# A two-attention, two-expert-layer block on one core: five steps moved around the expert layers, and the row maxima of the second attention handed over by PSUM bank

## What is computed

```python
x = x + attn_a(layernorm(x))
x = x + ffn(layernorm(x))
x = x + attn_b(layernorm(x))
x = x + ffn(layernorm(x))
```

```python
probs = softmax(q @ k.T)                      # 16 maps of 256 x 256
diff = probs[:, :, 0] - lam * probs[:, :, 1]
attn = (diff @ v) * rsqrt(mean(attn * attn) + 1e-5) * (1 - LAMBDA_INIT)
```

## Time and profile before

| | us |
|---|---|
| median of 3 runs | 936.07 (934.92 to 939.77) |
| the profiled execution, its own time | 938.77 |
| its span in the profile | 936.9 |
| PE busy | 830.4 (89%) |
| DVE busy | 697.6 (74%) |
| POOL busy | 573.9 (61%) |
| ACT busy | 555.4 (59%) |
| TensorE clock granted, mean | 0.947 |

### The profile page before, as it was taken

How to read it: one execution, slowest core, us unless ns; L and a number is a source line. 1 busy time by engine, 2 the same in 40 slices (tenths; PEclk the granted TensorE clock), 3 DMA queues, 4 the chain that set the end, 5 groups by cost and what they waited for, 6 DMA issues and landing times.

```text
span 936.9 us, 21558 instructions
## 1 busy us (share of the span) xinstructions
PE 830.4 (89%) x6976; PEld 578.8 (62%) x6976; DVE 697.6 (74%) x1916; ACT 555.4 (59%) x888; POOL 573.9 (61%) x666
## 2 busy tenths in 40 slices
PE   2799999987899999998789898898868889999998
PEld 1455555544687777787455555555534577777786
DVE  7588777785677777775778988889874587777764
ACT  1688887874544444444478888888864444444443
POOL 4677766681566676746347675767632776666652
PEclk8899999997999999999599999999985799999999
DMA  7000000001122222230000000000001122333331
GB/s 210 17 2 2 2 1 0 1 2 46 47 91 91 92 91 91 89 92 1 1 2 4 2 1 1 1 1 1 3 2 47 46 86 96 103 101 96 99 109 40
DMA packets 35702, 42.35 MB, mean 45 GB/s; under 512 B 5936, under 2 KB 18992, under 8 KB 35632
## 3 DMA queue, kind: packets, MB, share of 16 engines
q1 hardware_dynamic: 34048, 40.85, 14.3%
q10 hardware_dynamic: 1584, 0.62, 0.2%
HBM read 38.83 MB, written 2.36 MB: 44 GB/s over the span
## 4 chain that ended last, share of the span: by engine, by line
PE 49%; DVE 22%; POOL 11%; issue 10%; ACT 4%; DMA 3%; DVEq 1%; ACTq 0%; POOLq 0%
PE psum L1375 9%; DVE s_mxs L1137 6%; PE psum L394 6%; PE psum L1337 4%; PE psum L1338 4%; PE psum L1339 4%; DVE f_xe L1502 4%; PE psum L857 3%; POOL s_inv L1091 3%; PE psum L825 3%; PE psum L364 3%; PE psum L425 3%; PE psum L380 2%; PE psum L1393 2%; POOL s_rot L1106 2%
## 5 line engine op out<-in xcount | busy, mean ns | idle before, releaser
L1460 POOL TENSOR_TENSOR f_xe_lo<-f_xe,f_xe_hi 128x512 fp32r<-128x512 f32 x96 | 123.5, 1287 | 145.6 <-ACT f_xe_hi L1434 145.6
L1434 ACT ACTIVATE f_xe_hi<-f_xe 128x512 fp32r<-128x512 f32 x128 | 80.8, 631 | 207.9 <-DVE f_xe L1502 207.9
L1137 DVE TENSOR_REDUCE s_mxs<-psum 128x4 fp32r<-128x1024 f32 x128 | 155.8, 1219 | 30.4 <-PE psum L842 29.0
L1518 DVE TENSOR_TENSOR f_h<-psum,f_g 128x512 f32<-128x512 f32 x144 | 99.1, 688 | 88.4 <-ACT f_g L1419 70.2
L1375 PEld LDWEIGHTS psum<-w,f_h 128*128 128x128 f32 x1152 | 146.0, 191 | 29.7 <-DVE f_h L1518 21.4
L998 ACT ACTIVATE s_probs<-psum 128x1024 f32<-128x1024 f32 x128 | 131.2, 1025 | 50.0 <-PE psum L825 48.4
L1375 PE MATMUL psum<-w,f_h 128*128 128x128 f32 x1152 | 157.1, 279 | 3.8 <-DVE f_h L1518 2.5
L495 ACT ACTIVATE s_probs<-psum 128x1024 f32<-128x1024 f32 x128 | 126.0, 1023 | 28.8 <-PE psum L380 28.2
L1337 PE MATMUL psum<-f_xe_hi,w_hi 128*128 128x512 f32 x288 | 127.0, 441 | 1.1 <-POOL f_xe_lo L1460 1.1
L1338 PE MATMUL psum<-f_xe_hi,w_lo 128*128 128x512 f32 x288 | 114.4, 397 | 0.0
L1339 PE MATMUL psum<-f_xe_lo,w_hi 128*128 128x512 f32 x288 | 113.9, 396 | 0.0
(11 more groups left out here) (179 smaller groups left out, 1557.9 us busy)
## 6 DMA issues: line engine op xcount, KB each, us to landing
f_gt<-gates SPq DMA_DIRECT2D x128, 256.0 KB, 3.2
x<-in_x SPq DMA_DIRECT2D x8, 256.0 KB, 6.0
out<-x SPq DMA_DIRECT2D x8, 256.0 KB, 2.3
w<-in_w SPq DMA_DIRECT2D x3, 512.0 KB, 5.7
s_qt<-s_mt SPq DMA_DIRECT2D x32, 8.0 KB
rope_cos<-in_rope_cos SPq DMA_DIRECT2D x1, 256.0 KB, 3.6
rope_sin<-in_rope_sin SPq DMA_DIRECT2D x1, 256.0 KB, 3.5
gates<-f_sg SPq DMA_DIRECT2D x16, 16.0 KB
```

The source lines that it names most:

```text
L1137: dve.tensor_reduce(mxs[:, km % 2, p, r:r + 2, :, c:c + 1].bitcast(F32R), room(km, i).rearrange("p (r j s) -> p r j s", r=2, j=2), AX.X, A ...
L1460: pool.tensor_tensor(xe_lo[:, ring(e), :], src, xe_hi[:, ring(e), :], ALU.subtract).then_inc(xe_lo_pool.sem, 1)
```

## The change

Six edits:

1. **Maxima by bank.** PE writes the four products of a block bank by bank (u = 0, then u = 1) instead of half of each bank at a time, waits for DVE per bank, and signals each bank. DVE reduces each bank of 512 columns with an instruction of its own (two columns of `s_mxs`), 256 instructions instead of 128. The wait of PE for DVE moves from ahead of the block into it.
2. **LEAD, FF_LEAD.** The first lead-in slots (e = 0 to 4) stand after slots 2, 8, 10, 12, 14 of the last step but one instead of 5, 7, 9, 11, 13; x_turn moves from e = 0 to e = 1. So `f_xn` stands after slot 2 and `x_turn` after slot 8; both stood after slot 5.
3. **ACT in the expert layer.** The copy `f_xt` stands ahead of the high part `f_xe_hi` in the same slot.
4. **Normalising a chunk.** Three of the four `f_xn` in slot 3 and one in slot 4, instead of two and two.
5. **preceding** stands at slot 5 of step 0 of the second attention instead of slot 14 of step -1.
6. The semaphore counts that follow from 1.

```diff
-    mx_mm, mx_sb, mt_mm, mt_sb = ev("mx_mm", PAIRS), ev("mx_sb", PAIRS), ev("mt_mm", 2), ev("mt_sb", 2)
+    mx_mm, mx_sb, mt_mm, mt_sb = ev("mx_mm", 2 * PAIRS), ev("mx_sb", 2 * PAIRS), ev("mt_mm", 2), ev("mt_sb", 2)
...
-                pe.wait_ge(mx_sb.sem, mx_sb.upto(m, i - 1 if km == 0 and i else i))
-
-            def maxima(m, km, i, j):
-                c, q = i // 2 % 2, 2 * (i // 4) + j
-                for u in range(2):
+            def maxima(m, km, i, u):
+
+                pe.wait_ge(mx_sb.sem, mx_sb.upto(m, 2 * (i - 1 if km == 0 and i else i) + u - 1))
+                c = i // 2 % 2
+                for j in range(2):
+                    q = 2 * (i // 4) + j
                     r, o = 32 * (2 * (i % 2) + u), 512 * u + SEQ * j
                     ins = pe.matmul(room(km, i)[:, o:o + SEQ], qt[r:r + 24, km % 2, q, c * P:(c + 1) * P],
                                     kt[r:r + 24, km % 2, q, :], start=True, stop=True)
...
                     for m, km, i in blocks:
-                        ins = maxima(m, km, i, c)
-                        if c == 1:
-                            ins.then_inc(mx_mm.sem, 1)
+                        maxima(m, km, i, c).then_inc(mx_mm.sem, 1)
...
-                dve.wait_ge(mx_mm.sem, mx_mm.upto(m, i + 1))
-
-                dve.tensor_reduce(mxs[:, km % 2, p, r:r + 2, :, c:c + 1].bitcast(F32R),
-                                  room(km, i).rearrange("p (r j s) -> p r j s", r=2, j=2),
-                                  AX.X, ALU.max, negate=True).then_inc(mx_sb.sem, 1)
+                for u in range(2):
+                    dve.wait_ge(mx_mm.sem, mx_mm.upto(m, 2 * i + u + 1))
+                    dve.tensor_reduce(mxs[:, km % 2, p, r + u, :, c:c + 1].bitcast(F32R),
+                                      room(km, i)[:, 512 * u:512 * u + 512].rearrange("p (j s) -> p j s", j=2),
+                                      AX.X, ALU.max, negate=True).then_inc(mx_sb.sem, 1)
...
-LEAD = {(NSEQ - 2, 5): (0,), (NSEQ - 2, 7): (1,), (NSEQ - 2, 9): (2,), (NSEQ - 2, 11): (3,), (NSEQ - 2, 13): (4,),
+LEAD = {(NSEQ - 2, 2): (0,), (NSEQ - 2, 8): (1,), (NSEQ - 2, 10): (2,), (NSEQ - 2, 12): (3,), (NSEQ - 2, 14): (4,),
...
-FF_LEAD = {"x_turn": 0, "xt_sb": 1, "logits": 2, "best": 2, "index": 2, "masks": 2, "exp": 4, "sums": 4, "gates": 4}
+FF_LEAD = {"x_turn": 1, "xt_sb": 1, "logits": 2, "best": 2, "index": 2, "masks": 2, "exp": 4, "sums": 4, "gates": 4}
...
-                for m, km, next_e in inputs(n, k, e):
-                    high(m, km, next_e)
...
                     act.activation(xt[:, km % 2, :], T, ACT.Copy).then_inc(xt_sb.sem, 1)
+                for m, km, next_e in inputs(n, k, e):
+                    high(m, km, next_e)
...
-                    normalise(n + 2, (0, 1) if e == FF["norm"][0] else (2, 3))
+                    normalise(n + 2, (0, 1, 2) if e == FF["norm"][0] else (3,))
...
-            if n == -1 and h == 14 and preceding:
+            if n == 0 and h == 5 and preceding:
```

More of the change, by code:

```diff
@@ L885, in max_turn @@
             def max_turn(m, km, p):
-                pe.wait_ge(mx_sb.sem, mx_sb.upto(m, 4 * p + 4))
+                pe.wait_ge(mx_sb.sem, mx_sb.upto(m, 8 * p + 8))
                 if km + 1 < NSEQ:
```

## The result

The changed kernel takes **904.96 us** (median of 4 runs, 903.96 to 908.1) against 936.46 us for the kernel before on the same chip (4 runs, 934.92 to 939.77): ratio 0.9663, 95% interval 0.964 to 0.9687, so 31.5 us faster. The forecast was 904.0 with 891 to 924. The profiled execution took 905.03 us (span 902.7, mean granted clock 0.968), where the one before took 938.77. Lines of the code have moved by one: L825 stayed, the PE lines behind it up to the output projection are one higher (the maxima's products went from L842 to L843), all that follow are one lower (L998 is now L997, L1387 is L1386). Of the 11 executions of the kernel before in the second set of experiments one, of 2496.32 us at a granted clock of 1.00, is not compared with anything.

What follows compares the result with a forecast made beforehand. No one engine bounds the whole: PE bounds the expert layers, POOL's chain with DVE the second attention's loop. Terms -12 - 11 - 5 - 1 + 1 - 4 = -32 from 938.8 give 906.8, less 2.7: 904 us, range 891 to 924.

Steps and rivals of the forecast that it cites:

- a clock of 0.50 again between the last scores and the first experts: Sign of being wrong: half clock at the second seam, between second attention and second expert layer, in the profile after.
- Expert layers, -12: Both expert layers: PE's waits for f_xn and f_xt vanish in 12 chunk preparations, saving 12 us.
- Full removal is 12 x 1.15 = 13.8 us: Expert layers: upper end of the gain, 1.15 us of PE waits in each of 12 chunks; the lower end is 0.
- Second seam, -11: Lead into the second expert layer: without PE's gap the clock can stay up, saving 11 us; ends -2 and -15.
- a granted clock of 1.00 through the second: Sign of being right: PE's clock stays at full rate through the lead into the second expert layer.
- the clock falls again: Rival, 22%: the clock drops at the second seam, whose lead keeps about 3 of 11 us; 912 us total.
- First seam, -5: Lead into the first expert layer: less of 4.33 us PE idle and half-clock work, saving 5 us; ends 0 and -8.
- It now stands ahead of it: Lead into the first expert layer: f_xn, which took 3.82 us, now precedes POOL's 2.61 us w_lo.
- Start of the second attention, -1: Moving preceding shortens PE's 2.21 us idle before the first scores, saving 1 us; ends +1 and -3.
- Maxima in the loop, +1: Second attention's loop: split reductions against earlier PE work cost 0.1 us in each of 10 steps, +1 us.
- Maxima outside the loop, -4: About 20 second-attention blocks can fall from 1.95 to 1.66 us, saving 4 us; ends -6 and +1.
- The slower rival: Rival, 5%: bank order makes PE the bound in the second attention's loop; at 0.8 us more per block, 950 us.

Runs made afterwards that it cites:

- b_chunk: Kernel before with only the earlier f_xt copy and the three-and-one f_xn split in the expert layers: 919.70 us against 938.92, ratio 0.9791.
- b_copy: Kernel before with only ACT's f_xt copy put ahead of the high part, f_xn left two and two: 928.60 us against 936.42, ratio 0.9928.
- b_lead: Kernel before with only the LEAD and FF_LEAD slots changed: 926.67 us against 938.92, ratio 0.9858.
- a_wlo: The changed kernel with GpSimd's second w_lo moved from slot 5 to slot 15 of step 14, first attention: 902.22 us against 934.62 before, ratio 0.9641.
- change_again: The changed kernel itself, timed again beside the kernel before: 905.28 us against 934.62, ratio 0.9679.
- b_prec: Kernel before with only preceding moved to slot 5 of step 0 of the second attention: 935.70 us against 938.92, ratio 0.9978.
- a_rstd: The changed kernel with GpSimd's second-attention rstd moved from slot 14 to slot 3 of the next step: 899.46 us against 934.62 before, ratio 0.9624.
- b_bank: Kernel before with only the maxima handed over by bank and the counts for it: 934.42 us against 938.92, ratio 0.9938.

## Why the prediction was right, and where it was not

The sum was -32 us against the profiled execution; that one came out 33.7 shorter, the medians 31.5. The two largest gains came by the mechanisms named, but the terms were off in opposite directions: the expert layers gave some 5 us more than the sum has, the two seams some 7 less. That the sum came within 2 us is in part luck. One of the prediction's own signs of being wrong, "a clock of 0.50 again between the last scores and the first experts", did appear (0.57 on average over 703 to 715, so half clock for 10.3 of 12 us). Of its signs of being right, PE idle under 1 us before the first seam's turn did not (2.80 us).

- **Expert layers, -12.** Mechanism right: both waits gone, chunks with no gap. The term was mis-sized: 16.6 us in the ten periods, 16.9 to 22.3 by b_chunk's time. What failed is "Full removal is 12 x 1.15 = 13.8 us" as an upper end: 1.15 was idle time, and a wait of PE cost 0.2 to 0.3 us more than its idle time, twice per chunk. b_copy adds that in the second layer the two halves of the term don't divide as their rows do.
- **Second seam, -11.** `x_turn` waits for nothing and the logits' ranking no longer stops PE, as said. 8.1 us in the mean of five against nine executions (4.9 in b_lead, the only one with edit 2 alone), 12.4 in the two compared first; the text's ends (-2, -15) hold all three. The condition "a granted clock of 1.00 through the second" was not met: it fell three times, for 17 us in all. The rival "the clock falls again" describes what all nine executions do; it was priced at 3 of 11 kept, and 5 to 8 were kept, since the clock now comes back within the seam (17 to 34 us of half clock instead of 31 to 41).
- **First seam, -5.** The step that failed is "It now stands ahead of it". `f_xn` starts 0.8 us earlier in the span, but POOL reaches `w_lo` while it runs, and it had already been slowed from 0.34 to 0.76 us each by the passes before. The first `up` came 0.9 us earlier in the span, 1.5 counted from the same output projection (153.74, before 153.12), and 1.2 in the means of five executions each. a_wlo shows that -5 is about what a real removal brings: 4.8 us beside change_again, 5.3 in the means, 3.1 by the medians.
- **Start of the second attention, -1.** -1.5 to -1.9 in b_prec's trace, -2.1 (-4.6 to +0.4) in its time. The wait before the first scores went, and 1.87 us before the second block came: ACT's table load, which the prediction named as what leaves about 1 us to be had.
- **Maxima in the loop, +1.** 16.10 to 16.12 us, +0.2 in ten steps. POOL's chain was the bound (a_rstd). By length a block's two reductions are 2 x 0.681 - 1.219 = 0.14 us longer, back to back 1.29 against 1.23, 0.06. (The price per column was read from a reduction from PSUM and one of `s_sq`, which lies in SBUF; it came out right all the same, 0.68 us.) The Trainium skill (VectorE: DVE Perf Modes, errata section) has 120 cycles beside the elements for a source in PSUM. The estimate from it was 0.125 us on each block, 16 us in all. The trace agrees with the duration (0.14); a loss of 16 us is not there, since POOL's chain bounds the loop.
- **Maxima outside the loop, -4.** Between 2.0 (edit 1 undone in the change) and 5.8 (edit 1 alone), 2.9 at the two places that b_bank's turns of maxima show; with +1 for the loop on record the forecast for edit 1 was -3.
- **The slower rival**, bank order makes PE the bound, is out: a block that waits for nothing takes 0.44 us in both orders. The Trainium skill (TensorE: Matmul & The Clock Gate, Part 3) says that a weight load overlaps running matmuls only in another row group; the prediction worked out from it the stream of a product for each pair in one row group, and no row shows that. Yet the profile of the change, with PE busy 15.93 of 16.10 us, would have been read as that rival come true.

## What to carry to other kernels

Price a wait on TensorE by the distance between the instructions around it, with and without it, not by its idle time: here each was worth 0.2 to 0.3 us more than the row said, and waits inside a group of short products showed no idle at all and looked like work. Before moving a VectorE operation away from a GpSimd one, check where GpSimd will be by then; here moving the long GpSimd pass into a stretch where that engine was idle did what moving `f_xn` did not. Where the clock falls and comes back within a stretch, one trace says little about a term of 3 us: compare several executions of kernels that are alike there.
